# First layer's experts: token rows stationary, split weights moving, the down product one turn later

## The reference, cut to what matters

```python
logits = flat @ router_weight.T + router_bias
scores = jax.nn.softmax(logits, axis=-1)
topk_vals, topk_idx = jax.lax.top_k(scores, K)
gu = jnp.einsum('th,ehf->tef', flat, gate_up_proj) + gate_up_bias
gate = jnp.minimum(gu[..., :I], LIMIT)
up = jnp.clip(gu[..., I:], -LIMIT, LIMIT)
glu = gate * jax.nn.sigmoid(gate * ALPHA)
act = (up + 1.0) * glu
down = jnp.einsum('tei,eih->teh', act, down_proj) + down_bias
out = jnp.einsum('teh,te->th', down, w)
```

## Time and profile before

| what | value |
|---|---|
| median of 3 runs | 1749.59 us (1742.03 to 1760.26) |
| the profiled execution | 1749.45 us, span 1747.4 us |
| mean granted clock of TensorE | 0.969 |
| TensorE busy | 1636.7 us, 94% |
| VectorE, ScalarE, GpSimd busy | 61%, 38%, 20% |
| first layer's experts | from 608.9 to 788.2 us of the span |
| of these, turns 2 to 11 | 657.6 to 761.0 us |

### The profile page before, as it was taken

One profiled execution on the slowest core, in us unless ns is written; L12 is line 12 of the kernel. 1 busy time (PEld: TensorE's weight loads), 2 busy tenths in 40 slices (PEclk: granted clock), 3 DMA queues, 4 the chain that ended last, 5 costly groups with the idle time before them and its releaser, 6 DMA issues. The chain is left out here.

```text
span 1747.4 us, 23878 instructions
## 1 busy us (share of the span) xinstructions
PE 1636.7 (94%) x8996; PEld 1299.0 (74%) x8996; DVE 1070.6 (61%) x1653; ACT 656.4 (38%) x1242; POOL 354.9 (20%) x329
## 2 busy tenths in 40 slices
PE   8999999999998989988999998989899999899996
PEld 4899999999995777864556565758686667586782
DVE  4578777687684634455999997574526542232335
ACT  3454444444632111102544442144346533243441
POOL 1431333133121020011464543300200010000010
PEclk9999999999999989998998988999999989999998
DMA  5231223213114477548164552050101187496850
GB/s 172 78 114 57 75 96 99 72 57 114 57 43 151 178 273 261 201 138 304 62 204 149 176 196 105 34 195 1 46 6 49 36 339 256 171 335 225 309 198 31
DMA packets 111816, 247.30 MB, mean 142 GB/s; under 512 B 14518, under 2 KB 44230, under 8 KB 106950
## 3 DMA queue, kind: packets, MB, share of 16 engines
q1 hardware_dynamic: 103120, 226.52, 36.9%
q10 hardware_dynamic: 6006, 10.62, 1.7%
q0 software_dynamic: 2560, 8.39, 1.4%
HBM read 226.76 MB, written 18.75 MB: 140 GB/s over the span
## 5 line engine op out<-in xcount | busy, mean ns | idle before, releaser
L333 PE MATMUL x_ps<-x_cxt,x_qs 128*128 128x400 f32 (+1 forms) x1152 | 241.0, 354 | 1.2 <-PEq L365 1.2
L1298 PEld LDWEIGHTS e_ps<-e_xg,e_w 128*128 128x128 f32 x1792 | 208.1, 193 | 30.6 <-issue 27.9
L540 PE MATMUL x_ps<-x_cx,x_pt 128*128 128x386 f32 (+1 forms) x1248 | 228.6, 341 | 1.0 <-DVE x_o L628 1.0
L1298 PE MATMUL e_ps<-e_xg,e_w 128*128 128x128 f32 x1792 | 211.7, 277 | 10.5 <-issue 9.0
L540 PEld LDWEIGHTS x_ps<-x_cx,x_pt 128*128 128x128 f32 (+1 forms) x1248 | 218.5, 188 | 2.6 <-DVE x_o L628 1.2
L333 PEld LDWEIGHTS x_ps<-x_cxt,x_qs 128*128 128x128 f32 x1152 | 202.1, 189 | 2.8 <-issue 2.8
L2520 PE MATMUL x_s_ps<-x_cxt,x_qs 128*128 128x512 f32 (+1 forms) x384 | 141.3, 525 | 3.7 <-ACT x_sc L2641 1.7
L576 DVE TENSOR_TENSOR x_pt<-x_ps,x_pt 128x512 fp32r<-128x512 f32 (+1 forms) x128 | 74.5, 586 | 91.4 <-ACT x_pt L649 91.2
L2520 PEld LDWEIGHTS x_s_ps<-x_cxt,x_qs 128*128 128x128 f32 x384 | 67.9, 194 | 80.7 <-issue 79.0
L649 ACT CAST x_pt<-x_ps 128x512 fp32r<-128x512 f32 (+1 forms) x128 | 64.4, 505 | 157.6 <-PE x_ps L521 156.7
L1781 POOL DMA_INDIRECT e_w<-back,e_back_row x16 | 15.9, 993 | 387.8 <-ACTq L1686 383.6
(11 more groups left out here) (452 smaller groups left out, 2964.9 us busy)
## 6 DMA issues: line engine op xcount, KB each, us to landing
e_w<-in_L_ffn_W SPq DMA_DIRECT2D x16, 4096.0 KB, 14.5
x_cxt<-in_ctxT SPq DMA_DIRECT2D x8, 2401.5 KB, 8.6
x_cx<-in_ctx SPq DMA_DIRECT2D x8, 2304.0 KB
e_w<-in_L_ffn_gate_up_proj SPq DMA_DIRECT2D x8, 2048.0 KB, 8.7
x_stage<-in_ctxT SPq DMA_DIRECT2D x16, 768.0 KB, 4.3
x_stage<-in_ctx SPq DMA_DIRECT2D x16, 768.0 KB, 5.1
e_w<-in_L_ffn_down_proj SPq DMA_DIRECT2D x8, 1024.0 KB, 9.2
x<-in_ctxT SPq DMA_DIRECT2D x8, 768.0 KB, 4.6
```

The source lines that it names most:

```text
L333: last = nc.tensor.matmul(s_ps[:, n, 0:b - a], qs[:, u % 2, p, c, :], cxt[:, q, c, a:b], start=(m + c == 0), stop=(m + c == len(PARTS) + C ...
L540: last = nc.tensor.matmul(o_ps[:, 0:WIDE], pt[0:rows, p, t, :], cx[0:rows, q, t, :], start=(t + m == 0), stop=(t + m == KT - 1 + len(PARTS ...
L1298: last = nc.tensor.matmul(u_ps[:, g % 2, a * PER + n, :], w1[:, e % PAIR, m, a * hidden + c * P:a * hidden + (c + 1) * P], xg[:, m, :], st ...
```

## The change

In the first layer's experts the operands change places. The transposed rows, split in two parts (`xs`), are now stationary, and the weights move, 512 columns at a time, split in two parts as well (`w1s`, `w2s`). An up half (gate or up, 512 columns) is 4 x 3 float32r products, the down product another 4 x 3. The result of the up product has a token per partition, so the biases are rows, broadcast to all partitions by their loads (`load_rows`), and VectorE and ScalarE work on 128 x 512 (`tmp`). The hidden rows are then transposed on TensorE (`turn_hidden`), split (`high_hidden`, `low_hidden`) and multiplied in the middle of the next turn (`down_hidden`).

The weights are split by three engines: ScalarE casts the high parts of the up weights (`up_high`, four pieces of 128 x 1024), GpSimd subtracts the low parts (`up_low`), in the turn before the expert's own; the down weights' high parts are ScalarE's (two pieces of 128 x 1024) and the low parts VectorE's, at the end of the expert's first turn. Expert 0's up weights are split before the turns, among the router's work. SyncE loads a slot again as soon as its weights are split.

```diff
--- before.py
+++ after.py
@@ -1001,8 +1001,12 @@
     def load_up(self, sp, e):
         sp.dma_start(self.w1[:, e % PAIR, :, :], self.up_w[e].rearrange("(c p) n -> p c n", p=P)).then_inc(self.w1_in[e % PAIR], 16)
+    def load_rows(self, engine, e):
+        engine.dma_start(self.b1[:, e % PAIR, :], bcast(self.up_b[e])).then_inc(self.b1_in[e % PAIR], 16)
...
@@ -1082,9 +1087,15 @@
-        xg = core.sb(ctx, f"{name}_xg", [P, KC, P])
+        xg = None if gated else core.sb(ctx, f"{name}_xg", [P, KC, P])
-        tmp = core.sb(ctx, f"{name}_tmp", [P, 4, PER, P]) if gated else None
+        if gated:
+            xs = core.sb(ctx, f"{name}_xs", [P, 2, KC, P], F32R)
+            tmp = core.sb(ctx, f"{name}_tmp", [P, 3, hidden])
+            hid = core.sb(ctx, f"{name}_hid", [P, hidden])
+            w1s = core.sb(ctx, f"{name}_w1s", [P, PAIR, 2, KC, w1.shape[3]], F32R)
+            w2s = core.sb(ctx, f"{name}_w2s", [P, 2, HC, D], F32R)
+            hs = tuple(core.over(f"{name}_hs{p}", [P, HC, P], F32R, core.xt_at + p * HC * P * 4) for p in range(2))
...
@@ -1180,6 +1194,9 @@
+                if gated:
+                    weights.load_rows(sp, 0)
+                    weights.load_rows(sp, 1)
...
                 for e in range(E - PAIR):
-                    sp.wait_ge(w1_free, e + 1)
+                    if gated:
+                        sp.wait_ge(w1l_ready, (e + 1) * KC)
+                    else:
+                        sp.wait_ge(w1_free, e + 1)
                     weights.load_up(sp, e + PAIR)
-                    sp.wait_ge(w2_free, e + 1)
+                    if gated:
+                        sp.wait_ge(w2l_ready, (e + 1) * 2)
+                    else:
+                        sp.wait_ge(w2_free, e + 1)
                     weights.load_down(sp, e + PAIR)
...
+                def up_half(e, a):
+                    for m in range(KC):
+                        for p, q in PARTS:
+                            last = nc.tensor.matmul(ps[:, 4 + a, :], xs[:, p, m, :], w1s[:, e % PAIR, q, m, a * hidden:(a + 1) * hidden],
+                                                    start=(m == 0 and p + q == 0), stop=(m == KC - 1 and q == 1))
+                        if m == 0:
+                            one = last
+                    last.then_inc(up_ready, 1)
+                    return one
+                def turn_hidden(t):
+                    pe.wait_ge(h_ready, t)
+                    for c in range(HC):
+                        last = nc.tensor.transpose(x_ps[:, c, :], hid[:, c * P:(c + 1) * P], core.ident[:, :])
+                    last.then_inc(turned, 1)
+                def down_hidden(e, t):
+                    pe.wait_ge(w2l_ready, (e + 1) * 2)
+                    pe.wait_ge(hl_ready, t)
+                    pe.wait_ge(y_ready, t)
+                    for c in range(HC):
+                        for p, q in PARTS:
+                            last = nc.tensor.matmul(y_ps, hs[p][:, c, :], w2s[:, q, c, :],
+                                                    start=(c == 0 and p + q == 0), stop=(c == HC - 1 and q == 1))
+                    last.then_inc(down_ready, 1)
                 def gated_turn(e, t, fresh, q=1):
                     first = fresh and e == 0
+                    own = e == FINAL and not fresh
                     if fresh:
...
+                        pe.wait_ge(w1l_ready, (e + 1) * KC)
                     pe.wait_ge(xg_ready, t + 1)
+                    if own:
+                        turn_hidden(t)
                     if not first:
...
+                        pe.wait_ge(added, t * 2 - 1)
+                    one = up_half(e, 0)
                     if fresh and not first:
                         one.then_inc(w1_free, 1)
+                    if own:
+                        down_hidden(e, t)
+                    elif not first:
+                        turn_hidden(t)
                     if not first:
...
+                        pe.wait_ge(added, t * 2)
+                    up_half(e, 1)
+                    if first:
+                        idle(x_ps, IDLE)
+                    else:
+                        pe.wait_ge(hl_ready, t)
+                    pe.wait_ge(x_in, (t + 1) * 16)
+                    turn_rows()
+                    if own:
+                        spread(t, q - 1)
+                    elif not first:
+                        down_hidden(e - 1 if fresh else e, t)
                 def fresh_turn(e, t):
                     pe.wait_ge(w1_in[e % PAIR], (e // PAIR + 1) * 16)
...
                     t, q = turns(pe, lambda e, t, row: gated_turn(e, t, True), lambda e, t, n, row, q: gated_turn(e, t, False, q))
...
+                    pe.wait_ge(xg_ready, t + 1)
+                    turn_hidden(t)
+                    down_hidden(FINAL, t)
+                    pe.wait_ge(x_in, (t + 1) * 16)
                 else:
                     t, q = turns(pe, lambda e, t, row: fresh_turn(e, t), lambda e, t, n, row, q: more_turn(e, t, n, q))
...
+                def low_rows(t, source=x_ps):
+                    dve.wait_ge(xh_ready, t + 1)
+                    V.tensor_tensor(xs[:, 1, :, :], source, xs[:, 0, :, :].bitcast(F32), ALU.subtract).then_inc(xg_ready, 1)
+                def low_hidden(t):
+                    dve.wait_ge(hh_ready, t)
+                    V.tensor_tensor(hs[1][:, :, :], x_ps, hs[0][:, :, :].bitcast(F32), ALU.subtract).then_inc(hl_ready, 1)
                 def gated_turn(e, t, fresh, q=1):
+                    first = fresh and e == 0
+                    own = e == FINAL and not fresh
+                    if own:
+                        low_hidden(t)
...
+                    dve.wait_ge(up_ready, t * 2 + 1)
+                    V.tensor_tensor(tmp[:, 0, :], ps[:, 4, :], b1[:, e % PAIR, 0:hidden], ALU.add).then_inc(added, 1)
+                    dve.wait_ge(added, t * 2 + 1)
+                    V.tensor_scalar(tmp[:, 0, :], tmp[:, 0, :], LIMIT, None, ALU.min).then_inc(parts, 1)
+                    if own:
+                        take(t, e)
+                    elif not first:
+                        low_hidden(t)
+                    dve.wait_ge(up_ready, t * 2 + 2)
+                    V.tensor_tensor(tmp[:, 1, :], ps[:, 5, :], b1[:, e % PAIR, hidden:2 * hidden], ALU.add).then_inc(added, 1)
+                    dve.wait_ge(added, t * 2 + 2)
+                    V.tensor_scalar(tmp[:, 1, :], tmp[:, 1, :], LIMIT, -LIMIT, ALU.min, ALU.max).then_inc(parts, 1)
+                    low_rows(t + 1)
+                    dve.wait_ge(parts, t * 3 + 2)
+                    V.scalar_tensor_tensor(tmp[:, 1, :], tmp[:, 1, :], 1.0, tmp[:, 0, :], ALU.add, ALU.mult).then_inc(parts, 1)
+                    dve.wait_ge(parts, t * 3 + 3)
+                    dve.wait_ge(sig_ready, t + 1)
+                    V.tensor_tensor(hid[:, :], tmp[:, 1, :], tmp[:, 2, :], ALU.mult).then_inc(h_ready, 1)
+                    if not first and not own:
+                        take(t, e - 1 if fresh else e)
+                    if fresh:
+                        for half in range(2):
+                            part = slice(half * HC // 2, (half + 1) * HC // 2)
+                            dve.wait_ge(w2h_ready, e * 2 + (half + 1))
+                            V.tensor_tensor(w2s[:, 1, part, :], w2[:, e % PAIR, part, :], w2s[:, 0, part, :].bitcast(F32),
+                                            ALU.subtract).then_inc(w2l_ready, 1)
...
+                def up_high(e, k):
+                    nc.scalar.copy(w1s[:, e % PAIR, 0, k, :], w1[:, e % PAIR, k, :]).then_inc(w1h_ready, 1)
+                def down_high(e):
+                    act.wait_ge(w2_in[e % PAIR], (e // PAIR + 1) * 16)
+                    for half in range(2):
+                        part = slice(half * HC // 2, (half + 1) * HC // 2)
+                        nc.scalar.copy(w2s[:, 0, part, :], w2[:, e % PAIR, part, :]).then_inc(w2h_ready, 1)
+                if gated:
+                    act.wait_ge(w1_in[0], 16)
+                    for k in range(KC):
+                        up_high(0, k)
...
+                def high_hidden(t):
+                    act.wait_ge(turned, t)
+                    nc.scalar.copy(hs[0][:, :, :], x_ps).then_inc(hh_ready, 1)
+                def high_rows(t, source=x_ps):
+                    act.wait_ge(x_ready, t + 1)
+                    nc.scalar.copy(xs[:, 0, :, :], source).then_inc(xh_ready, 1)
                 def rows_back(t):
                     act.wait_ge(y_out, t * 16 + 16)
                     act.sem_inc(all_out, 1)
                 def store(t, row):
...
+                    act.wait_ge(y_ready, t + TAKES)
                     act.dma_start(back[bass.ds(row * MORE, P), :], y[:, :]).then_inc(y_out, 16)
                 def gated_turn(e, t, fresh):
                     first = fresh and e == 0
+                    ahead = fresh and e + 1 < E
+                    if ahead:
+                        act.wait_ge(w1_in[(e + 1) % PAIR], ((e + 1) // PAIR + 1) * 16)
```

(35 more changed lines are left out.)

114 lines of the change are left out of this document (33 added, 81 removed).

## The result

The changed kernel takes 1782.5 us (median of 4 runs, 1777.1 to 1797.3), the kernel before 1746.7 (4 runs): a ratio of 1.022, 95% interval 1.016 to 1.028. The change makes the kernel about 36 us slower; the forecast was 1773, that is +23.

What follows compares the result with a forecast made beforehand. TensorE, busy 94% of the span, was taken to bound the kernel. Start +19.2, nine turns +2.1 and last turn +1.8 summed to +23.1 us on 1749.45, so 1773 us, range 1751 to 1788.

Steps and rivals of the forecast that it cites:

- the nine turns: From the start of turn 2 to that of turn 11: 105.5 us against 103.4, +2.1 us.
- the last turn: From turn 11's start to the end of the last addition: 28.5 to 29 us against 27.2, +1.8 us.
- Start: Stage's beginning to turn 2: held one-hot tiles, late stored rows and late expert 1 weights start turn 2 +19.2 us later.
- the row at 60.96: Profile row before the change: a 64-column tensor_scalar stands until the GpSimd instruction beside it is over; basis for the held case.
- In a fresh turn GpSimd's first subtraction starts 2.0 us in: In the nine turns: TensorE frees the slot at 0.9 us, then ScalarE's cast takes 1.05.
- its second and third wait for VectorE's held operations: In a fresh turn, GpSimd's second and third subtractions also wait for ScalarE; the last ends at 12.35 us.
- TensorE's own term: TensorE's work per turn: 9.3 us where it needed 11.0 to 11.5.
- one addition, the one-hot rows, the low part and the last down product: In the last turn, after spreading: 4.9 us, before the weighted rows at 5.9.
- (1): GpSimd and VectorE instructions lie beside each other, VectorE not held: 1755 us; chance 0.22.
- (2): TensorE sets the pace in all nine turns, if GpSimd's pieces take under 1.5 us: 1746 us; chance 0.09.
- (3): Clock falls after TensorE's waits in fresh turns, up to four turns cost 2.7 us more each: +11, 1784 us; chance 0.12.
- Costs put at nothing: Broadcast bias rows, 0.5 MB an expert more, and weight loads hide; the rest of the kernel has the same instructions.

Runs made afterwards that it cites:

- the experiment with the stores first: Changed kernel with GpSimd's four subtractions for expert 0 moved behind its eight stores of rows; one run, 1788.2 us.
- the early load: Changed kernel with expert 1's weights loaded before SyncE waits for the stored rows; 1776.1 us, 1.012 of the kernel before.
- the unneeded work: Changed kernel with 8-column GpSimd subtractions for experts 2 to 7, each followed by a 128x1024 subtraction nobody waits for; turns 2 to 11 took 106.0 us.
- the short low parts: Changed kernel with GpSimd's subtraction cut to 8 of 1024 columns for experts 2 to 7; 1762.7 us, 1.006 of the kernel before.
- the idle products: Changed kernel with 40 idle products ahead of TensorE's wait for the split in fresh turns of experts 2, 3, 6 and 7; 1783.6 us.

## Why the prediction was right or wrong

**Direction: right.** Slower by over 1% was given 0.55, and 2.2% was measured. The time, 1782.5 us, is near the upper end of the range, and that it lies inside owes something to luck: the stage cost 41.9 us more and not 23.1, and 9.0 us of that were given back by stages whose instructions are the same. The 18.8 us missing in the stage are two terms, the nine turns (14.4) and the last turn (4.5).

**Start, +19.2 forecast, +19.1 measured: right, for the reasons given; the agreement to 0.1 is luck.** The hold delayed the stored rows by 6.7 us (the experiment with the stores first), the wait of the weights behind them is worth 11 (the early load), turn 1 began 9.0 us after the weights landed (658.58), against 9.6. Counted from the stage's beginning, the second expert's load was issued 1.8 us later than forecast (the scores came late at the lower clock); the landing (8.0 us), the casts and turn 1 (10.9 us) were 0.5 to 0.7 us shorter each, which made that up. In this execution the one-hot tiles did not stretch, but the copies and tensor_scalars ahead of them did, with 4 to 32 columns; in six other profiles the tiles did, as forecast. By the row at 60.96 I had looked only at the operations that I knew to be large; a hold counts instructions, not columns.

**Nine turns, 105.5 forecast, 119.9 measured: the failed step.** "In a fresh turn GpSimd's first subtraction starts 2.0 us in": it starts 5.1 us in (683.58 in turn 2), and 4.7 and 4.6 us in in turns 6 and 8, since ScalarE reaches the casts only 3.9 us into turn 2. (In turns 3, 4 and 9, behind a fresh turn, it starts 3.5 us in, near the 3.4 of the forecast.) Its store (679.78) stands behind the taking of the rows of the turn before, and 2.3 us pass behind the store ([5.95 <-issue] in the cast's row); the sum had 1 us for all this. Then "its second and third wait for VectorE's held operations" was right in kind and too small: a piece takes 2.48 us in the mean of 32, not 2.2. The forecast turns of 12.45 and 13.85 were 15.3 and 15.7, and 14.8 and 15.6 in the second pair. Turns 4 and 10, forecast at 10.3 and 9.3, took 12.6 and 11.1: there the missing 4.1 us are the clock, since their first halves took 5.48 and 4.51 us instead of 2.9. The experiments split the stretch roughly into 93.8 without the split (7 of them late weights), +12 by the hold and +14 by the wait for the split. TensorE's own term was a little small: 9.6 us a turn and not 9.3 (the products stream at 0.24 us, and the low part of the hidden rows is waited for).

**Last turn, +1.8 forecast, +6.3 measured: mis-sized.** Its timeline on ScalarE and TensorE:

```profile
801.91 0.58 ACT L1769 CAST e_hs<-e_ps 128x512 fp32r<-128x512 f32 x1 [1.59 <-DMA back<-e_y]
```
```profile
803.51 3.04 PE L1360 MATMUL e_ps<-e_w2s,e_hs 128*128 128x512 f32 x12 [1.72 <-issue]
...
818.26 4.40 PE L1360 MATMUL e_ps<-e_w2s,e_hs 128*128 128x512 f32 x12 [4.68 <-issue]
```

Up to the end of the spreading (813.14) it took 14.8 us, as forecast (14.5), although the hidden rows' cast stands behind the wait for a store (1.59 us). The failed term is the next, 4.9 us for "one addition, the one-hot rows, the low part and the last down product": it took 9.5 us, to 822.66. By rows at hand it was too small from the start, since the addition alone is 2.48, the low part 0.69 and twelve products 2.8. Beyond that the last down product came after a wait of 4.68 us and ran at the lower clock (4.40 us instead of 3.04), and I had taken it at full speed. No experiment was made on this term.

**Rivals.** (1), instructions beside each other, is excluded by the 2.33 us and by the unneeded work. (2), TensorE sets the pace, is what the short low parts made, but for turn 4. (3), the clock in the new gaps, did happen: first halves of 5.13, 5.48, 5.42 and 4.51 us instead of 2.9, 8.9 us in all. Priced at +11, it was worth 1.8 to 5.2 in the stretch when the idle products took it away; where the split sets the turn, it ended hardly earlier. I had it as a case beside the forecast, but it adds to it. Its 1784 us is nearest to the measured time, yet the clock is the smaller part of the 18.8 us missing in the stage: the last turn is 4.5, and in turns 2 and 8, where no slow first half stands, late casts and longer pieces make 5.2.

**Costs put at nothing.** The bias rows and the weights were never waited for in a turn: right at this pace, no longer at 9.2 us a turn (the 6.50 us of the short low parts). That the rest of the kernel costs the same since its instructions are the same: right within 9 us for this change, wrong as a rule, as the 15.6 us of the next stage show.

## What to carry to other kernels

Before work is handed to GpSimd beside a chain on VectorE, count that chain's copies, tensor_scalars and two-input operations in SBUF, not their columns: each may wait for a whole instruction of the other. Look where the helper's first step stands in its own queue, behind which store, wait and branch, since a split in four steps over two engines begins no earlier than that. Measure an unchanged stretch in more than one execution before a few us in it are called a gain. And when a gain shown by the marks of a stage does not reach the total, compare the granted clock in the stages behind it before looking for another cause.

## What the runs showed of the hardware that I had not expected

- A copy of 8 columns and tensor_scalars of 4 and 32 columns waited for GpSimd as large ones did (1.43, 2.32 and 1.50 us; the copy of 4 columns, which began as one piece ended, took 0.16). The MATCH_REPLACE8 operations between them, also in SBUF, took 0.16 us each beside the pieces and were not held. The Trainium skill ("SBUF — State Buffer", section "SBUF: two separate sides") makes the shared port pair an exclusive lock for a two-port operation or one with two SBUF inputs. The trace agrees, down to these sizes; and with the first operand in PSUM all four operations ran at 0.69 to 0.70 beside GpSimd.
- ScalarE needed about 2 us (1.9 to 2.3) between the store of one turn and its first cast in the next, with nothing to wait for in the profile (in the row with [5.95 <-issue]). Whether it is the branch, the reading of the counts or the queue was not tried.
- Two waits of TensorE of 1.7 us, in a stage that otherwise kept it busy, were followed by over 10 us at 1.2 GHz in some kernels and not in others, though the instructions are the same. What differs between them was not found; idle products in the waits kept the clock at 1.00 in the one profile, and all four runs (1770.9 to 1783.5 us) were faster than the four without (1791.6 to 1798.9), measured at another time.
